# Three output parts: the clip waited for by itself, the first stage's rise folded into constants, side sums moved between stages

## The reference

```
def _derivative(q, p, drive, coupling, bias):
    i_couple = jnp.tanh(q) @ coupling.T
    dq = q - q ** 3 / 3.0 - p + drive + i_couple + bias
    dp = EPSILON * (q + ALPHA - BETA * p)
    return (dq, dp)

def _rk4_step(q, p, drive, coupling, bias):
    dq1, dp1 = _derivative(q, p, drive, coupling, bias)
    dq2, dp2 = _derivative(q + 0.5 * DT * dq1, p + 0.5 * DT * dp1, drive, coupling, bias)
    dq3, dp3 = _derivative(q + 0.5 * DT * dq2, p + 0.5 * DT * dp2, drive, coupling, bias)
    dq4, dp4 = _derivative(q + DT * dq3, p + DT * dp3, drive, coupling, bias)
    q_next = q + DT / 6.0 * (dq1 + 2 * dq2 + 2 * dq3 + dq4)
    p_next = p + DT / 6.0 * (dp1 + 2 * dp2 + 2 * dp3 + dp4)
    q_next = jnp.clip(q_next, -CLAMP, CLAMP)
    p_next = jnp.clip(p_next, -CLAMP, CLAMP)
```

## Time and profile before

| what | value |
|---|---|
| median of 3 runs | 5724.95 us |
| the profiled run's own time | 5725.47 us |
| its span, first to last instruction | 5723.7 us |
| VectorE busy | 5294.6 us, 93% |
| TensorE matmul busy | 4535.9 us, 79% |
| ScalarE busy | 2605.5 us, 46% |
| share of the chain that ended last | VectorE 67%, TensorE 17%, ScalarE 8%, issue 6% |
| mean granted TensorE clock | 0.993 |

### The profile page before, as it was taken

One profiled execution on the slowest core, in us unless ns is written; L12 is line 12 of the kernel. 1 busy time (PEld: TensorE's weight loads), 2 busy tenths in 40 slices (PEclk: granted clock), 3 DMA queues, 4 the chain that ended last, 5 costly groups with the idle time before them and its releaser, 6 DMA issues.

```text
span 5723.7 us, 849105 instructions
## 1 busy us (share of the span) xinstructions
PE 4535.9 (79%) x394763; PEld 4119.4 (72%) x394763; DVE 5294.6 (93%) x33615; ACT 2605.5 (46%) x12040; POOL 5.7 (0%) x16
## 2 busy tenths in 40 slices
PE   7887777777777777777777777777777777777777
PEld 3437777777777777777777777777777777777777
DVE  5568999999999999999999999999999999999999
ACT  3334444444444444444444444444444444444444
POOL 0000000000000000000000000000000000000000
PEclk8999999999999999999999999999999999999999
DMA  5100000000000000000000000000000000000000
GB/s 218 47 16 1 0 7 0 7 0 0 7 0 7 0 7 0 7 0 0 7 0 7 0 7 0 0 7 0 7 0 7 0 0 7 0 7 0 7 0 7
DMA packets 11599, 57.09 MB, mean 10 GB/s; under 512 B 2616, under 2 KB 2616, under 8 KB 8512
## 3 DMA queue, kind: packets, MB, share of 16 engines
q1 hardware_dynamic: 11056, 55.84, 2.5%
q10 hardware_dynamic: 528, 1.05, 0.1%
HBM read 40.11 MB, written 16.78 MB: 10 GB/s over the span
## 4 chain that ended last, share of the span: by engine, by line
DVE 67%; PE 17%; ACT 8%; issue 6%; DMA 0%; DVEq 0%; SPq 0%; ACTq 0%
DVE xb L677 35%; PE ps L636 12%; DVE xb L837 12%; DVE tanh_parts L677 7%; ACT xb L449 5%; DVE xb L856 4%; ACT xb L498 2%; DVE drive L677 2%; DVE xb L963 2%; PE ps L525 2%; ACT tanh_parts L455 1%; DVE xb L952 1%; DVE xb L959 1%; PE ps L543 1%; PE ps L580 1%
## 5 line engine op out<-in xcount | busy, mean ns | idle before, releaser
L636 PE MATMUL ps<-coup,tanh_parts 128*16 128x96 f16 (+1 forms) x393408 | 4184.6, 202 | 1110.4 <-ACT tanh_parts L455 590.8
L636 PEld LDWEIGHTS ps<-coup,tanh_parts 128*16 128x16 f16 x393408 | 3957.6, 89 | 1338.1 <-ACT tanh_parts L455 703.7
L677 DVE SCALAR_TENSOR_TENSOR xb<-xb 128x64 f32<-128x64 f32 (+2 forms) x17412 | 2936.9, 209 | 198.9 <-ACT xb L498 92.6
L449 ACT ACTIVATE xb<-xb 128x24 f32<-128x24 f32 (+1 forms) x4098 | 940.5, 230 | 2499.8 <-DVE xb L677 2396.1
L837 DVE STREAM_TRANSPOSE xb<-ps 128x96 f32<-128x96 f32 (+1 forms) x6144 | 1508.4, 261 | 32.6 <-PE ps L636 6.8
L677 DVE SCALAR_TENSOR_TENSOR tanh_parts<-xb,tanh_parts 128x24 f16<-128x24 f32 (+1 forms) x4098 | 738.9, 180 | 15.5
L498 ACT ACTIVATE xb<-xb 128x64 f32<-128x64 f32 x2048 | 499.1, 244 | 64.2
L455 ACT ACTIVATE tanh_parts<-xb 128x24 f16<-128x24 f32 (+1 forms) x2050 | 470.3, 229 | 64.6
L856 DVE SCALAR_TENSOR_TENSOR xb<-xb 128x64 f32<-128x64 f32 x2049 | 452.8, 221 | 0.0
L467 ACT ACTIVATE tanh_parts<-xb 128x24 f16<-128x24 f32 (+1 forms) x2048 | 357.2, 221 | 121.0
L461 ACT ACTIVATE xb<-xb 128x64 f32<-128x64 f32 x1024 | 262.5, 256 | 95.9 <-DVE xb L677 95.0
(11 more groups left out here) (69 smaller groups left out, 720.3 us busy)
## 6 DMA issues: line engine op xcount, KB each, us to landing
xb<-in_x SPq DMA_DIRECT2D x8, 2048.0 KB, 7.9
drive<-in_x_pt SPq DMA_DIRECT2D x8, 2048.0 KB, 24.6
out_pt<-drive SPq DMA_DIRECT2D x16, 1024.0 KB, 5.4
drive<-in_coupling_t SPq DMA_DIRECT2D x8, 512.0 KB, 11.6
mask_v<-in_cond SPq DMA_DIRECT2D x8, 132.0 KB
probs<-in_wo ACTq DMA_DIRECT2D x1, 1024.0 KB, 5.5
w_qkv<-in_wq SPq DMA_DIRECT2D x1, 64.0 KB, 3.7
w_qkv<-in_wk SPq DMA_DIRECT2D x1, 64.0 KB, 5.2
```

Source lines behind the costliest of these rows:

```text
L449: nc.scalar.activation(cols(tanh_sb, CHUNKS[j]), cols(q, CHUNKS[j]), ACT.Tanh, scale=unit_of[1.0])\
L636: last = nc.tensor.matmul(product(s, o)[SQ * g:SQ * g + ROWS, :], tanh_parts[:, s % 2, k, :], coup[:, k, part, g, n0:n1, :].rearrange("p c ...
L677: return V.scalar_tensor_tensor(out=out, in0=a, scalar=factor, in1=c, op0=ALU.mult, op1=op1)
```

## The change

`rise = q1 - q0` is no longer computed. Its three users take `q1` and have the part with `q0` in other constants; the third stage's start takes it as `q_part`, a multiple of q1 that ScalarE now makes with one more instruction a step, behind `q_share` (L509 of the changed kernel). The clip signals `side_ready` itself: `g0`, moved ahead of `z`, waits for that, and so does ScalarE's square. `q_sum_g0` moves from the middle of stage 0 to between the cubic and the base behind stage 3, `p_sum_g0` to where `rise` stood, and `trace` from the end of stage 1 to between the first transpose and `q_of` in stage 1, where `p_sum_g0` stood.

```diff
-Q_KEPT = 1 - THIRD - Q_STEP[0] * Q_STEP[1] - (CURVE * OFFSET - STEP[3] - THIRD)
-P_ALL = 1 + P_SUM[2]
+Q_KEPT = 1 - THIRD - Q_STEP[0] - Q_STEP[0] * Q_STEP[1] - (CURVE * OFFSET - STEP[3] - THIRD)
+P_ALL = 1 + P_SUM[1] + P_SUM[2]
+Y_PART = single(1 + DT * RISE * G1[1])
...
                     if following == 0:
-                        act.wait_ge(clipped, act.snap(now >> 2))
+                        act.wait_ge(side_ready, now)
...
                         nc.scalar.activation(q_share[:, :], q_st[0][:, :], ACT.Copy, scale=Q_KEPT)\
                           .then_inc(q_share_ready, STAGES)
+                        nc.scalar.activation(q_part[:, :], q_st[1][:, :], ACT.Copy, scale=1 - Y_PART)\
+                          .then_inc(q_part_ready, STAGES)
...
-            def z_of_third():
-                axpy(z3[:, :], rise[:, :], -DT * RISE * G1[1], y_less[:, :]).then_inc(z_ready, 1)
-            def rise_of_first():
-                V.tensor_tensor(rise[:, :], q_st[1][:, :], q_st[0][:, :], ALU.subtract)
+            def z_of_third(now):
+                dve.wait_ge(q_part_ready, now)
+                axpy(z3[:, :], y_less[:, :], Y_PART, q_part[:, :]).then_inc(z_ready, 1)
...
-                axpy(q_sum[1][:, :], q_sum[0][:, :], DT / 2 / Q_SUM[1], rise[:, :])
+                axpy(q_sum[1][:, :], q_sum[0][:, :], DT / 2 / Q_SUM[1], q_st[1][:, :]).then_inc(side_ready, 1)
...
-            def g0_of():
+            def g0_of(now):
+                dve.wait_ge(side_ready, now)
                 axpy(g0[:, :], p_st[:, :], -BETA, q_st[0][:, :])
...
-                axpy(p_sum[1][:, :], rise[:, :], P_SUM[1] / P_ALL, p_sum[0][:, :])
+                axpy(p_sum[1][:, :], q_st[1][:, :], P_SUM[1] / P_ALL, p_sum[0][:, :])
...
                 V.tensor_scalar(q_st[0][:, :], q_raw[:, :], bounds[:, 0:1], bounds[:, 1:2], ALU.max, ALU.min)\
-                 .then_inc(clipped, 1)
+                 .then_inc(side_ready, 1)
...
                 if s == 1:
-                    p_sum_g0()
+                    trace((now - 2) * (COLS // STAGES))
...
                     y_less_g0()
-                    q_sum_g0()
                     z_of_second()
...
                     with_first_part(1, z_first_part, z2, made)
+                    p_sum_g0()
                     cubic_of(1, made)
-                    rise_of_first()
+                    drive_step_of(now_at)
                     base_of(1, made)
-                    drive_step_of(now_at)
...
                     less_q_of()
-                    trace((made - 3) * (COLS // STAGES))
...
                 if s == 3:
-                    dve.wait_ge(square_ready, made)
+                    g0_of(made - 1)
                     z_of_first()
-                    g0_of()
                     with_first_part(0, z_first_part, z, made)
                     cubic_of(0, made)
+                    q_sum_g0()
                     base_of(0, made)
```

More of the change, by code:

```diff
@@ L202, in build @@
         q_share = state()
-        rise = state()
+        q_part = state()
         q_sum = [state() for k in range(3)]
@@ L275, in build @@
         z_ready = sem("z_ready")
+        q_part_ready = sem("q_part_ready")
         side_ready = sem("side_ready")
-        clipped = sem("clipped")
         traced = sem("traced")
@@ L878, in y_of @@
             def y_of():
-                axpy(y[:, :], drive_p[:, :], DT, q_st[0][:, :]).then_inc(side_ready, 1)
+                axpy(y[:, :], drive_p[:, :], DT / Y_PART, q_st[0][:, :]).then_inc(side_ready, 1)
             def y_less_g0():
-                axpy(y_less[:, :], g0[:, :], -DT * RISE * G1[0], y[:, :])
-            def z_of_third():
-                axpy(z3[:, :], rise[:, :], -DT * RISE * G1[1], y_less[:, :]).then_inc(z_ready, 1)
-            def rise_of_first():
-                V.tensor_tensor(rise[:, :], q_st[1][:, :], q_st[0][:, :], ALU.subtract)
+                axpy(y_less[:, :], g0[:, :], -DT * RISE * G1[0] / Y_PART, y[:, :])
+            def z_of_third(now):
+                dve.wait_ge(q_part_ready, now)
+                axpy(z3[:, :], y_less[:, :], Y_PART, q_part[:, :]).then_inc(z_ready, 1)
             def q_sum_g0():
@@ L924, in forecast_first @@
                 axpy(forecast[:, :], less_q[:, :], 1 / 3, q_st[3][:, :]).then_inc(forecast_ready, 1)
-            def g0_of():
+            def g0_of(now):
+                dve.wait_ge(side_ready, now)
                 axpy(g0[:, :], p_st[:, :], -BETA, q_st[0][:, :])
             def p_sum_g0():
-                axpy(p_sum[0][:, :], g0[:, :], P_SUM[0] / P_ALL, q_st[0][:, :], ALU.subtract)\
-                 .then_inc(side_ready, 1)
+                axpy(p_sum[0][:, :], g0[:, :], P_SUM[0] / P_ALL, q_st[0][:, :], ALU.subtract)
             def p_sum_r1():
-                axpy(p_sum[1][:, :], rise[:, :], P_SUM[1] / P_ALL, p_sum[0][:, :])
+                axpy(p_sum[1][:, :], q_st[1][:, :], P_SUM[1] / P_ALL, p_sum[0][:, :])
             def p_sum_q2():
@@ L954, in look_ahead @@
             def look_ahead(into, at):
-                axpy(drive_b[into][:, :], drive_cols[:, bass.ds(at, COLS)], inv_unit[:, 0:1], bias_b[:, :]).then_inc(side_ready, 1)
+                axpy(drive_b[into][:, :], drive_cols[:, bass.ds(at, COLS)], inv_unit[:, 0:1], bias_b[:, :])
             def drive_less_p(now_at):
@@ L985, in _ @@
             base_of(0, 1)
-            g0_of()
+            axpy(g0[:, :], p_st[:, :], -BETA, q_st[0][:, :]).then_inc(setup, 1)
+            dve.wait_ge(setup, 11)
+            q_sum_g0()
             def until_rest(s, now_at, now):
@@ L1013, in until_rest @@
                     q_sum_r1()
-                    z_of_third()
+                    z_of_third(now)
                 if s == 2:
```

## The result

The changed kernel took 5656.56 us, the median of four runs (5651.19 to 5657.6), against 5724.9 before: a ratio of 0.9879, 95% interval 0.9862 to 0.9896, or 68 us less. The forecast was 5653. The profiled run took 5655.78 with a span of 5654.0, 69.7 less than before. Over the 512 steps, from the first to the last transpose, the time fell from 5281.8 to 5215.4, by 66.4. Nearly all of the rest, 3.2, lies ahead of the first transpose (435.2 before, 432.0 after), where the change only adds a wait and an instruction.

A forecast was written before the change was run, and what follows sets the result against it. A ring of 2048 products bounds the kernel, not one engine; only longer turnarounds count. Terms -0.32 - 0.14 + 0.05 + 0.07 + 0.07 save 0.28 a pass, 72 us: 5653 us, range 5612 to 5697.

The forecast's parts named there:

- The floor of 2.50 us: Shortest turnaround between TensorE products, already reached by three; excess above it totals 0.61 a pass, at most 156 us to win.
- the earliest place: Earliest start of a stage's first transpose on VectorE, 1.34 us behind the start of its product.
- Stage 0: Clip's signal and new order start the first transpose 0.15 earlier; turnaround 2.51, taken as 2.50: -0.16 twice a pass.
- The added wait: In stage 0, z's reader now waits for z directly in front: 0.25 apart, against 0.135 for neighbours without a wait.
- Stage 2: With the trace gone from ahead of its first transpose, both turnarounds reach the floor: -0.04 and -0.10 a pass.
- The other 0.07 at the branch: Behind stage 0, chunk 1's rest part comes 0.41 instead of 0.34 behind the product, lengthening the branch turnaround: +0.07.
- The trace's new price: Between first transpose and q_of in stage 1, taken as 0.16, 0.05 more than now; bounds 0.11 and 0.28.
- the rivals with 0.28 and over 0.34: Trace in stage 1 costs its whole 0.28: 5697 us, chance 0.11; from about 0.34 on, slower: 5756 us, chance 0.07.
- the slower outcome: In stage 1, q_of is held until the trace has written drive: 31 us slower, 5756 us, chance 0.07.
- The rival with the floor everywhere: Stage 3 keeps 2.50 and the trace costs only a plain instruction: 0.40 a pass saved, 5623 us, chance 0.15.
- that of the renamed wait: Clipped q or the square comes over 0.25 later, so stage 0 keeps 2.66: about 5720 us, chance 0.05.
- The count theory: VectorE's time goes by its number of instructions, 0.135 us x 512 = 69 us for each a step; order and waits free.

The follow-up runs named there:

- E7: Changed kernel with trace moved to stage 2, p_sum_g0 back behind stage 1's transpose, p_sum_r1 in stage 1's wait, z ahead of g0: 5609.51 us.
- E1: Kernel before with the clip's part alone: g0 first, waiting for the clip's own signal, then z; rise and trace unchanged: 5665.25 us.
- E3: Changed kernel with one extra 64-column VectorE instruction a step in stage 0's wait for its tanh: 5654.8 us.
- E4: Changed kernel with the same extra VectorE instruction a step on stage 0's path, between q_sum_g0 and the base: 5704.19 us.
- E2: Changed kernel with g0 waiting for ScalarE's square again instead of the clip: 5773.52 us.
- E5: Changed kernel with the trace back at the end of stage 1 and its new place left empty: 5666.86 us.
- E6: Changed kernel with ScalarE's new copy q_part made twice a step, the second into a spare tile: 5654.24 us.
- E8: E7's order with four steps instead of two in a pass of VectorE's and ScalarE's loops: 5596.63 us.

## Why the prediction was right, point by point

**The floor of 2.50 us** held: three of the eight turnarounds after the change are 2.49 to 2.50, and E7 brings stage 0 there too. What the working did not say is that the floor has slack. On the timeline of the kernel before, the first transpose of stage 3 is this one:

```profile
3006.05 0.28 DVE L837 STREAM_TRANSPOSE xb<-ps 128x96 f32<-128x96 f32 x1
```

It stands 1.42 behind its product at 3004.63, 0.08 behind the earliest place of 1.34, and the stage still turned in 2.50. So a first transpose costs only what it comes later than some 1.44, which is an estimate: the floor's 2.50 less the 1.06 from stage 0's first transpose to the next product. That is why stage 0, 0.26 behind the earliest place, lost only 0.16, and stage 2, 0.20 behind it, only 0.10; the limit of 1.34 in E1's expectation is too strict. E3 and E4 show what the ring charges for: an instruction that falls into a wait is free, one that makes the first transpose later is paid.

**Stage 0** was forecast with the first transpose 1.45 behind the product, and stands at 1.46. The turnaround is 2.51 to 2.52, as the working said; the step that rounded it to the floor's 2.50 was 0.01 to 0.02 too kind, twice a pass, some 5 us. Over the steps the gain was 66.4 of the 72 that were forecast; that the result lies only 3.6 us above the forecast is owed in part to the 3.2 us that the stretch ahead of the steps took less in this run, which the forecast did not reckon with and which is luck. E1 shows the clip's part, the wait taken out less the wait put in, to be 57 of the 68 us; E2 shows that with the wait for the square the new order loses against the kernel before.

**The added wait** between z and its reader costs 0.12 (0.61 against 0.49), as the row of cubic and base said, and E7 takes it away again. The rule of the Trainium skill (VectorE: DVE Perf Modes, "The DRAIN you can't avoid") that a semaphore between neighbours costs nothing extra was not borne out for these instructions of 64 columns. Nor was their number what counted: see E3 and E4.

**Stage 2** went to the floor, as forecast. What the trace won there was nearly all given back: 0.04 in each stage 3 and 0.05 in the branch's stage 1, which the forecast had priced at 0.07 for both and 0.05. E5 shows the balance, some 13 us. The other 0.07 at the branch came as worked out, with the rest part 0.41 behind its product; E1, where the trace has not moved, has 2.73 there.

**The trace's new price**, the widest unknown, is 0.16, the same as `look_ahead` in the same place. So the rivals with 0.28 and over 0.34 are out, and the slower outcome with them. The rival with the floor everywhere is out by stage 3, 2.53, and that of the renamed wait by stage 0's 2.52 and by the idle time on the square, which is gone.

**q_part** was hidden as said, but the reason was counted wrongly on the safe side: I gave it its length of 0.24 out of 0.30 of idle time, with 0.06 left. By E6 it takes up 0.15, and two of them fit.

**`rise`** was costed at nothing, and E5 against E1 shows that its removal and the moves of the two sums together brought nothing; by itself it was not tested. The count theory would have put it at 69 us, which is just what the whole change brought; the agreement was chance, as E1, E3 and E5 show.

Left open: why the wait behind the branch is 0.28 to 0.30 wherever it stands; no run here changes it, E7 and E8 only place it better or have fewer.

## What to carry to other kernels

Where engines hand work round in a ring, write down for each stage how late its critical instruction starts behind the event that it could start on, and how much of that lateness the stage bears at no cost. In this kernel an instruction or a wait was worth what it took from the lateness beyond that and nothing more, though its engine was 93% busy. Wait for the producer itself and not for a later engine that happens to wait for it too, and put an independent instruction between a producer and its reader on the same engine. A stage that is brought to its floor hands its side work on later to the next one, so price the stage behind it too.

## What the runs showed that was not expected

The recorded length of an instruction is not its price; the prediction still took it for one with `q_part` and as the upper bound of the trace. The trace is 0.28 us long at the end of a row of others and 0.24 behind a transpose; a 64-column SCALAR_TENSOR_TENSOR is 0.22 in a row and 0.18 behind a transpose; ScalarE's copy is 0.24 and takes up 0.14 to 0.15. The distance to the next start was the right price each time, but that too goes by the place: the trace takes up 0.20 ahead of stage 2's transpose and 0.16 behind stage 1's.
